# Rows of negated maxima in a fused attention block: written by a DMA per head instead of by products with the identity

## The chip, the cores and the metric

The kernel runs on one core of one Trainium2 chip. The metric is the device time of one execution in microseconds (us).

## The reference

One transformer block over a batch of 8 sequences of 256 tokens with 128 features, and a context of 8 x 1601 tokens with 96 features:

```python
attn_in = _adaln(x, cond, ...)                       # layer norm, scaled and shifted by cond
x = _attn(attn_in, attn_in, sa_wq, sa_wkv, sa_wo, sa_bo) + x
cross_in = _adaln(x, cond, ...)
ctx_n = _ln(context, ca_lnc_w, ca_lnc_b)
x = _attn(cross_in, ctx_n, ca_wq, ca_wkv, ca_wo, ca_bo) + x
ffn_in = _adaln(x, cond, ...)
x = gelu(ffn_in @ ff_w1 + ff_b1) @ ff_w2 + ff_b2 + x

# _attn: 16 heads of 64
q, k = _rope(q, sq, cq), _rope(k, sk, ck)
sim = einsum('bhnd,bhmd->bhnm', q, k) * DH ** (-0.5)
o = einsum('bhnm,bhmd->bhnd', softmax(sim), v)
```

The softmax takes the maximum of each query's scores away before the exponential. The kernel computes that maximum for every query and head.

## The kernel before, in words

All data stay on the chip with features on partitions. The work goes in **steps**: a step J is one sequence and one pair of heads. There are 64 steps of self-attention (class of settings `SELF`) and then 64 of cross-attention (`CROSS`), eight steps (the eight pairs) to a sequence. After them comes the feed-forward part.

What each engine does in a step, and in which order, is written by hand as a string of words (lines 83 to 97). A word names an action; a digit behind it is a part of the step (a chunk of 512 keys, a unit of 2 tiles of 124 keys); `+n` says that the action is done for the step n ahead of the current one, `+-1` for the one behind. Each engine runs its words strictly in order; semaphores tie the engines together. The five strings are those of TensorE, VectorE, ScalarE, GpSimd and SyncE, in that order. SyncE does nothing but issue transfers.

The words that matter here, with their lines:

- `t`, `c`, `r` in self-attention (VectorE, lines 918 to 938) are the rotation of queries and keys. `t` multiplies the projected values by the sines into `turned`; SyncE's word `x` (`self_swap`, line 473) swaps neighbouring rows of `turned` into `swapped` with two transfers SBUF to SBUF; `r` adds `swapped` to get the rotated `QK`. In cross-attention the same is `kt`, `kc`, `ka` with SyncE's `k` for the keys, and `qt`, `qc`, then `qa` on GpSimd, with SyncE's `q` for the queries.
- `w` (SyncE, line 463 and 494) loads the projection weights of a later step, two transfers; `wo` in cross-attention loads output weights, one.
- `a` (TensorE, lines 1172 and 1310) computes scores with queries on the partitions of PSUM, for the maximum alone. VectorE reduces them: in self-attention `am` writes `nmx` (line 942), the negated maxima with queries on partitions; in cross-attention `am0` to `am6` write parts and `nm` writes `nmxc` (line 1044).
- `m` (TensorE, `max_rows`, lines 1184 and 1332) turns these into rows. Four products with the identity, the maxima broadcast over 64 columns as weights, write each head's 256 negated maxima into the PSUM bank `XB`, on 64 partitions alike. ScalarE's word `mr` (`rows_of_max`) copies the bank to `MX`.
- `s` (TensorE, lines 1193 and 1343) computes the scores proper, with keys on the partitions, in three products of high and low parts, and a fourth that adds the negated maximum: `share`, filled with 1/64, times `MX`. ScalarE's `e` takes the exponential.
- `p`, `sum`, `o` (TensorE) are the products with the values, the sum of the exponentials and the output projection. GpSimd adds the exponentials up (`c1` to `c6` and `cf` in cross-attention) before `sum`. In self-attention `o` does work only at the last step of a sequence, 16 products at once (line 1249).
- The bank `XB` serves `m`, `sum` and `o` in turn, in cross-attention also `q` and `v`. `x_free` makes each wait for the reader of the use before it.

`RAMP` strings and `RAMP_*` tables say which words of the first cross-attention steps are done in the last ones of self-attention.

Of the kernel before, what the change touches and what calls it, by code (L numbers as in the profile page):

```python
# [12 lines left out]
D = 128  # L13
# [11 lines left out]
class Stage:  # L25


    def __init__(self, name, pe, dve, act, pool, sp, xuses=("m", "sum", "o")):
# [14 lines left out]
class Cross(Stage):  # L43


    def __init__(self, name, rows, keys, tile, chunk, pe, dve, act, pool, sp):
        super().__init__(name, pe, dve, act, pool, sp, ("q", "v", "m", "sum", "o"))
# [18 lines left out]
def block_kernel(nc, xT_in, cT_in, ctx_in, cols_in, cols96_in, ada_in, packs, w1_in, w2_in,  # L66
# [22 lines left out]
    CROSS = Cross("ca", DC, M, 124, 512,  # L89
# [11 lines left out]
    with ExitStack() as ctx:  # L101
# [38 lines left out]
        nmx = sb("nmx", [D, 2, 2])  # L140
        mxc = sb("mxc", [D, 2, 2, len(CROSS.chunks)])
        nmxc = sb("nmxc", [D, 2, 2])
# [80 lines left out]
        class SelfSteps:  # L223

            def __init__(self, a):
                n = a.name
                self.w = [sem(f"{n}_weights_loaded{i}") for i in range(UNROLL)]
                self.wo = sem(n + "_wo_loaded")
                self.qk = sem(n + "_projected")
                self.t = sem(n + "_turned")  # L230
                self.c = sem(n + "_cosines")
                self.swap = [sem(f"{n}_swapped{i}") for i in range(SLOTS)]
                self.r = sem(n + "_rotated")
                self.h = sem(n + "_high")
# [5 lines left out]
                self.mt = sem(n + "_max_rows")  # L240
                self.mr = sem(n + "_max_rows_copied")
                self.s = sem(n + "_scores")
                self.e = sem(n + "_exp")
                self.pv = sem(n + "_pv")
                self.oe = sem(n + "_o_read")
                self.f = sem(n + "_fold")
                self.sum = sem(n + "_sum")
                self.inv = sem(n + "_sum_inverse")
                self.ot = sem(n + "_o_scaled")
                self.y = sem(n + "_y")  # L250
                self.added = sem(n + "_added")

        class CrossSteps:

            def __init__(self, a):
# [22 lines left out]
                self.mt = sem(n + "_max_rows")  # L278
                self.mr = sem(n + "_max_rows_copied")
# [95 lines left out]

        def halves(tile):
            return tile.rearrange("p (a n) -> p a n", n=N)
# [38 lines left out]

        RAMP_PE = {61: "k0", 62: "k1 q0", 63: "k2"}
# [38 lines left out]
        def _(sp):  # L456
# [31 lines left out]
            run_steps(SELF, in_order(SELF.sp, {"w": self_weights, "x": self_swap}))  # L488
# [30 lines left out]

            def cross_weights_of(J, _):  # L520
                cross_weights(J, J % PAIRS)
# [4 lines left out]
            do = {"q": swap_q, "k": swap_k, "w": cross_weights_of, "wo": cross_out_weights_of}  # L526
            ramp = "w w+1 k0 k1 q k2"
            run_ramp(ramp, do)
            run_steps(a_, in_order(a_.sp, do, ahead(ramp)))
# [12 lines left out]
        def _(pool):  # L542
# [11 lines left out]
            pool.memset(share[:, :].bitcast(F32), 1.0 / DH).then_inc(s_rows, 1)  # L554
# [146 lines left out]
        def _(act):  # L701
# [26 lines left out]
            def self_attention(do):  # L728
# [11 lines left out]
                def rows_of_max(J, _):  # L740
                    wait(act, z.mt, J + 1)
                    wait(act, z.s, J - 1)
                    copy(MX[J % 2][:, :], XB[:, 0:N]).then_inc(z.mr, 1)

# [44 lines left out]
                words = {"cn": context_squares, "ca": context_out, "h": high_parts, "ve": read_v, "mr": rows_of_max,  # L789
# [3 lines left out]
            def cross_words():  # L793
# [21 lines left out]
                def rows_of_max(J, _):  # L815
                    wait(act, x.mt, times(J, 1) + 1)
                    wait(act, x.s, times(J, NU) - NU)
                    copy(MX[J % 2][:, :], XB[:, 0:N]).then_inc(x.mr, 1)

# [13 lines left out]
                do = {"qh": high_q, "kh": high_k, "ve": read_v, "mr": rows_of_max, "e": exponentials, "oe": read_o}  # L833
                return do

            def cross(do):
# [5 lines left out]
                ramp = ("table0 square0 kh2 square1 kh3 ve0 square2 ve1 root0 mr table1 e0 ve2 e1 kh0+1 out0 qh+1 e2 "  # L842
# [23 lines left out]
            act.wait_ge(s_rows, 3)  # L866
# [5 lines left out]
        def _(dve):  # L872
# [44 lines left out]
            def self_attention(do):  # L917
# [21 lines left out]
                def maximum(J, _):  # L939
                    wait(dve, z.a, J + 1)  # L940
                    wait(dve, z.mt, J)
                    dve.tensor_reduce(nmx[:, :, :], MP[:, :, :].rearrange("p h (t n) -> p h t n", n=N), AX.X, ALU.max,  # L942
                                      negate=True).then_inc(z.am, 1)
# [37 lines left out]
            def cross_words():  # L981
# [59 lines left out]
                def maximum(J, _):  # L1041
                    wait(dve, x.am, times(J, NM) + NM)
                    wait(dve, x.mt, times(J, 1))
                    dve.tensor_reduce(nmxc[:, :, :], mxc[:, :, :, :], AX.X, ALU.max, negate=True
                                      ).then_inc(x.nm, 1)
# [46 lines left out]
        def _(pe):  # L1092
# [26 lines left out]
            RAMP = ("a0 zsum0 zp0 a1 mean0 mean1 k3 a2 zo0 a3 var0 a4 var1 mean2 v0 a5 v1 var2 a6 m k0+1 s0 v2 q+1 s1 k1+1 "  # L1119
# [20 lines left out]
            def self_attention(do):  # L1140
# [3 lines left out]
                readers = {"m": (z.mr, lambda K, k: K + 1),  # L1144
                           "sum": (z.ot, lambda K, k: K + 1),
# [108 lines left out]
                words = {"qk": project, "v": project_v, "a": max_scores, "m": max_rows, "s": scores, "p": products,  # L1254
# [4 lines left out]
            def cross_words():  # L1259
# [4 lines left out]
                           "m": (x.mr, lambda K, k: K + 1), "sum": (x.ot, lambda K, k: K + 1),  # L1264
# [47 lines left out]
                def max_scores(J, u):  # L1312
# [11 lines left out]
                    for t in range(2) if last else (u % 2,):  # L1324
                        for h in range(2):
                            at = t * N if last else 0
                            ins = pe.matmul(MP[:, h, at:at + w], QH[J % UNROLL][half(h), t * D:(t + 1) * D],  # L1327
                                            KH[J % 2][half(h), lo:lo + w], start=True, stop=True)
                    ins.then_inc(x.mp, 1)

                def max_rows(J, _):
                    wait(pe, x.nm, times(J, 1) + 1)
                    x_free(uses, readers, J, ("m", 0))
                    for t in range(2):
                        for h in range(2):
                            ins = pe.matmul(XB[half(h), t * D:(t + 1) * D],
                                            nmxc[:, t, h:h + 1].broadcast_to([D, DH]), ident[:, :],
                                            start=True, stop=True)
                    ins.then_inc(x.mt, 1)

                def scores(J, c):
                    r, i = J % UNROLL, J % 2
                    wait(pe, x.kl, times(J, NK) + a_.chunk_of(c) + 1)
                    if c == 0:
                        wait(pe, x.ql, times(J, 1) + 1)
                        wait(pe, x.mr, times(J, 1) + 1)
# [36 lines left out]
                def output(J, _):  # L1383
# [4 lines left out]
                    for h in range(2):  # L1388
# [4 lines left out]
                      "m": max_rows, "s": scores, "p": products, "sum": sums, "o": output}  # L1393
# [87 lines left out]
            pe.wait_ge(s_rows, 3)  # L1481
# [61 lines left out]
```

## Time and profile before

| | |
|---|---|
| median of 3 runs | 1983.65 us (1982.58 to 1987.21) |
| the profiled execution, its own time | 1985.08 us |
| its span in the trace | 1983.3 us |
| mean granted clock of TensorE | 0.991 of full |
| TensorE busy | 1915.2 us (97%) |
| VectorE busy | 1570.7 us (79%) |
| GpSimd busy | 1265.8 us (64%) |
| ScalarE busy | 984.3 us (50%) |
| transfers issued by SyncE | queue busy 17.8% of 16 engines' span |

Names in the profile: PE is TensorE, PEld its weight load, DVE VectorE, ACT ScalarE, POOL GpSimd, SP SyncE (SPq its queue of transfers). The span runs from the first to the last instruction; the profiled execution's time is 1.8 us more. A busy share is a mean over stages that are limited by different things.

### The profile page before, as it was taken

The page shows a single profiled execution, that of the slowest core. Times are in us where ns is not written, and L with a number is a line of the kernel's source. Part 1 is how long each engine was busy: PE and PEld are TensorE (multiplying, and loading weights), DVE is VectorE, ACT ScalarE, POOL GpSimd, SP SyncE. Part 2 cuts the span into 40 slices and gives each one's busy share as a digit, 9 for nine tenths or more (in the row PEclk, how much of TensorE's full clock was granted, in tenths as well). Part 3 has the DMA queues.
Part 4 walks back from the last instruction along what each step waited for, and adds up shares of the span by engine and source line. Part 5 has one row for each costly group of instructions (what it writes and reads, how often), then busy time and mean ns, then how long its engine had stood idle before and what let it go on. Part 6 is the DMA issues. An engine that isn't in the chain of part 4 may idle for free.

```text
span 1983.3 us, 53782 instructions
## 1 busy us (share of the span) xinstructions
PE 1915.2 (97%) x20840; PEld 1327.3 (67%) x20840; DVE 1570.7 (79%) x2291; ACT 984.3 (50%) x1587; POOL 1265.8 (64%) x819
## 2 busy tenths in 40 slices
PE   6989998988999999999999999999999999999998
PEld 3666776754667767666676766666676677676663
DVE  4888888887888888888888888888888888888852
ACT  3555555544544545544455454445445445555455
POOL 6667655423676766667677667666766766766662
PEclk8999999998999999999999999999999999999999
DMA  5222223211111111111111111111111111111110
GB/s 192 76 83 77 76 82 102 76 50 48 50 50 56 51 56 58 49 49 50 56 51 59 55 50 50 55 52 55 57 51 50 50 55 52 56 58 49 46 35 22
DMA packets 110871, 118.90 MB, mean 60 GB/s; under 512 B 26528, under 2 KB 74784, under 8 KB 110624
## 3 DMA queue, kind: packets, MB, share of 16 engines
q1 hardware_dynamic: 110624, 115.46, 17.8%
q8 instruction: 173, 2.83, 0.6%
q14 instruction: 74, 0.61, 0.1%
HBM read 36.71 MB, written 1.05 MB: 19 GB/s over the span
## 4 chain that ended last, share of the span: by engine, by line
PE 77%; POOL 6%; DMA 6%; DVE 5%; issue 3%; SPq 1%; ACT 1%; DVEq 0%; POOLq 0%; ACTq 0%
PE S L1356 19%; PE OB L1370 17%; PE PB L1295 9%; PE PB L1308 8%; PE S L1327 7%; POOL psum_acc L682 4%; DMA swapped<-turned 4%; DMA qswapped<-qturned 2%; PE PB L1379 2%; PE PB L1280 2%; PE OB L1231 1%; PE PB L1249 1%; PE S L1203 1%; PE PB L1389 1%; DVE nmx L942 1%
## 5 line engine op out<-in xcount | busy, mean ns | idle before, releaser
L682 POOL TENSOR_TENSOR psum_acc<-psum_acc,P 124x1024 f32<-124x1024 f32 (+1 forms) x320 | 690.2, 2157 | 113.7 <-ACT P L825 96.5
L825 ACT ACTIVATE P<-S 124x1024 f32<-124x1024 f32 (+1 forms) x448 | 431.7, 964 | 462.8 <-PE S L1356 461.0
L1039 DVE TENSOR_REDUCE mxc<-S 128x2 f32<-128x1024 f32 x384 | 468.7, 1221 | 85.6 <-PE S L1327 85.0
L1370 PE MATMUL OB<-P,V 124*64 124x256 f32 (+1 forms) x3328 | 428.5, 381 | 0.0
L675 POOL TENSOR_TENSOR psum_acc<-P 124x1024 f32<-124x1024 f32 x64 | 152.4, 2381 | 318.8 <-ACT P L825 318.8
L1370 PEld LDWEIGHTS OB<-P,V 124*64 124x64 f32 (+1 forms) x3328 | 223.5, 136 | 132.5 <-issue 38.6
L1356 PE MATMUL S<-QH,KH 64*124 64x256 f32 (+1 forms) x1664 | 254.5, 302 | 1.7 <-ACT P L825 1.7
L703 ACT ACTIVATE V<-PB 124x512 f32<-124x512 f32 (+1 forms) x320 | 156.7, 490 | 172.1 <-PE PB L1169 83.2
L1004 DVE TENSOR_TENSOR turned<-PB,rope 128x512 f32<-128x512 f32 (+1 forms) x256 | 146.0, 570 | 118.7 <-PE PB L1295 118.5
L1356 PE MATMUL S<-QH,KL 64*124 64x256 f32 (+1 forms) x1664 | 234.4, 277 | 0.0
L1356 PE MATMUL S<-MX,share 64*124 64x256 f32 (+1 forms) x1664 | 234.4, 277 | 0.0
L1356 PE MATMUL S<-QL,KH 64*124 64x256 f32 (+1 forms) x1664 | 234.4, 277 | 0.0
L1308 PE MATMUL PB<-kv_w,ctxT_all 96*64 96x128 f32 (+2 forms) x3328 | 231.5, 276 | 0.0
L1356 PEld LDWEIGHTS S<-QH,KH 64*124 64x124 f32 (+1 forms) x1664 | 153.7, 181 | 108.4 <-issue 108.2
L1308 PEld LDWEIGHTS PB<-kv_w,ctxT_all 96*64 96x64 f32 (+2 forms) x3328 | 185.3, 134 | 58.3 <-issue 37.4
L1295 PE MATMUL PB<-ctxT_all,kv_w 96*64 96x512 f32 (+1 forms) x1024 | 222.9, 514 | 0.9 <-DVE KL L1025 0.6
L1327 PE MATMUL S<-KH,QH 64*128 64x512 f32 (+1 forms) x1024 | 199.8, 407 | 10.2 <-DVE mxc L1039 7.1
L1017 DVE TENSOR_TENSOR PB<-PB,swapped 128x512 f32<-128x512 f32 (+1 forms) x256 | 147.7, 577 | 59.5 <-DMA swapped<-turned 58.2
L1356 PEld LDWEIGHTS S<-QH,KL 64*124 64x124 f32 (+1 forms) x1664 | 154.6, 182 | 12.2
L703 ACT ACTIVATE KH<-PB 128x512 fp32r<-128x512 f32 (+1 forms) x256 | 128.4, 502 | 61.8 <-DVE PB L1017 61.2
L1356 PEld LDWEIGHTS S<-MX,share 64*124 64x124 f32 (+1 forms) x1664 | 154.7, 181 | 0.0
L1356 PEld LDWEIGHTS S<-QL,KH 64*124 64x124 f32 (+1 forms) x1664 | 154.4, 181 | 0.0
(169 smaller groups left out, 2999.3 us busy)
## 6 DMA issues: line engine op xcount, KB each, us to landing
swapped<-turned SPq DMA_DIRECT2D x512, 128.0 KB, 2.1
kv_w<-sa_kv_dram SPq DMA_DIRECT2D x64, 128.0 KB, 2.3
qswapped<-qturned SPq DMA_DIRECT2D x128, 64.0 KB, 1.9
kv_w<-ca_kv_dram SPq DMA_DIRECT2D x64, 96.0 KB, 2.2
ctxT_all<-ctx_dram SPq DMA_DIRECT2D x8, 624.0 KB, 5.1
q_w<-sa_wq_dram SPq DMA_DIRECT2D x64, 64.0 KB, 2.0
q_w<-ca_wq_dram SPq DMA_DIRECT2D x64, 64.0 KB, 2.0
o_w<-ca_wo_dram SPq DMA_DIRECT2D x64, 64.0 KB, 2.0
```

What stands on the lines that cost most here:

```text
L675: pool.tensor_tensor(acc, P_of(J, 0)[0:rows], P_of(J, 1)[0:rows], ALU.add).then_inc(x.acc, 2)
L682: pool.tensor_tensor(acc, acc, P_of(J, c)[0:rows, :, 0:w], ALU.add).then_inc(x.acc, 1)
L703: return act.activation(out, in_, ACT.Copy)
L825: act.activation(P_of(J, c)[0:rows, :, 0:w], SP[0:rows, :, 0:w], ACT.Exp, scale=SCALE).then_inc(x.e, 1)
L1004: dve.tensor_tensor(turned[c][:, 0:w], KB[c % 2][:, 0:w], rope[:, M + lo:M + lo + w], ALU.mult).then_inc(x.kt, 1)
L1017: dve.tensor_tensor(KB[c % 2][:, 0:w], KB[c % 2][:, 0:w], swapped[c][:, 0:w], ALU.add).then_inc(x.ka, 1)
L1039: dve.tensor_reduce(mxc[:, t, :, c:c + 1], MP[:, :, 0:w], AX.X, ALU.max).then_inc(x.am, 1)
L1295: ins = pe.matmul(KB[c % 2][half(h), 0:w], kv_w[J % UNROLL][0:DC, half(h)], ctxT_all[0:DC, at:at + w], start=True, stop=True)
L1308: ins = pe.matmul(XB[a:b, k * PAIR:(k + 1) * PAIR], ctxT_all[0:DC, lo + a:lo + b], kv_w[J % UNROLL][0:DC, PAIR:2 * PAIR], start=True, stop ...
L1327: ins = pe.matmul(MP[:, h, at:at + w], QH[J % UNROLL][half(h), t * D:(t + 1) * D], KH[J % 2][half(h), lo:lo + w], start=True, stop=True)
L1356: ins = pe.matmul(SP[0:w, h, k * N:(k + 1) * N], keys[half(h)], queries[half(h), :], start=(n == 0), stop=(n == len(terms) - 1))
L1370: ins = pe.matmul(OB[half(h), 0:N], Vb[J % 2][0:w, t, half(h)], P_of(J, c)[0:w, h, k * N:(k + 1) * N], start=(t == 0), stop=(t == len(a_.t ...
```

## The change

`max_rows` on TensorE, its copy `rows_of_max` on ScalarE, and their two semaphores go, in both stages. In their place SyncE has a new word `mx`: for each of the two heads one transfer from `nmx` (or `nmxc`), 128 partitions with two numbers each, into one row of `MX` of 256 numbers, on partition 0 or 64. So that the two numbers of a partition are neighbours in the row, the maximum scores are computed with queries 2p and 2p+1 on partition p: the weights of `a` are read with a step of two (`t::2`) in place of 128 queries in a row. `share` becomes 1.0 and the other rows of `MX` are zeroed once, so that the fourth product of `s` adds one row. `nmx` and `nmxc` get two buffers each. The words `w`, `w+1` and `k0` of SyncE's first cross-attention steps move into the last self-attention steps.

```diff
     SELF = Stage("sa",
-                 "qk+3 v+2 sum+-1 p+-1 s a+2 ct m+1 o+-1 n",
+                 "qk+3 v+2 sum+-1 p+-1 s a+2 ct o+-1 n",
                  "r+2 am+1 t+3 rc+-1 dv+-1 c+3 ad+-1 cn n",
-                 "e mr+1 ca cn ve+3 h+3 oe",
+                 "e ca cn ve+3 h+3 oe",
                  "l+2 cp f cq",
-                 "w+3 x+2")
+                 "w+3 x+2 n+1 mx+1")
     CROSS = Cross("ca", DC, M, 124, 512,
-                  "a3 k0+1 v3+-1 p1+-1 a4 s3+-1 q+1 p2+-1 a5 s4+-1 v0 n0 k1+1 s5+-1 a6 v1 n1 k2+1 p3+-1 m n2 "
+                  "a3 k0+1 v3+-1 p1+-1 a4 s3+-1 q+1 p2+-1 a5 s4+-1 v0 n0 k1+1 s5+-1 a6 v1 n1 k2+1 p3+-1 n2 "
...
-                  "e3+-1 e4+-1 ve0 kh0+1 e5+-1 ve1 qh+1 mr n0 kh1+1 e6+-1 ve2 n1 e0 oe+-1 kh2+1 e1 n2 e2 "
+                  "e3+-1 e4+-1 ve0 kh0+1 e5+-1 ve1 qh+1 n0 kh1+1 e6+-1 ve2 n1 e0 oe+-1 kh2+1 e1 n2 e2 "
...
-                  "w+2 k3 k0+1 q+1 k1+1 wo k2+1")
+                  "w+2 k3 k0+1 q+1 k1+1 mx wo k2+1")
...
+        def max_to_rows(sp, negated, rows, semaphore):
+
+            for h in range(2):
+                sp.dma_start(rows[h * DH:h * DH + 1, :].bitcast(F32),
+                             negated[:, h, :].bitcast(F32)).then_inc(semaphore, 16)
...
+            def self_max(J, _):
+                wait(sp, z.am, J + 1)
+                wait(sp, z.s, J - 1)
+                max_to_rows(sp, nmx[J % 2], MX[J % 2], z.mr[J % 2])
...
+            def cross_max(J, _):
+                wait(sp, x.nm, J + 1)
+                wait(sp, x.s, times(J, NU) - NU)
+                max_to_rows(sp, nmxc[J % 2], MX[J % 2], x.mr[J % 2])
...
-            pool.memset(share[:, :].bitcast(F32), 1.0 / DH).then_inc(s_rows, 1)
+            pool.memset(share[:, :].bitcast(F32), 1.0).then_inc(s_rows, 1)
+            for i in range(2):
+                pool.memset(MX[i][:, :].bitcast(F32), 0.0).then_inc(s_rows, 1)
...
-                            ins = pe.matmul(MP[:, h, t * N:(t + 1) * N], high(J, 0, t * D, t * D + D)[half(h)],
+                            ins = pe.matmul(MP[:, h, t * N:(t + 1) * N], high(J, 0, 0, N)[half(h), t::2],
                                             high(J, 1, 0, N)[half(h)], start=True, stop=True)
...
-                def max_rows(J, _):
-                    wait(pe, z.am, J + 1)
-                    x_free(uses, readers, J, ("m", 0))
-                    for t in range(2):
-                        for h in range(2):
-                            ins = pe.matmul(XB[half(h), t * D:(t + 1) * D],
-                                            nmx[:, h, t:t + 1].broadcast_to([D, DH]), ident[:, :],
-                                            start=True, stop=True)
-                    ins.then_inc(z.mt, 1)
...
                 def scores(J, _):
                     wait(pe, z.l, J + 1)
-                    wait(pe, z.mr, J + 1)
+                    wait(pe, z.mr[J % 2], J // 2 * 32 + 32)
```

The order of SyncE's transfers in a self-attention step, before (names: `swapped<-turned` is the word `x`, `kv_w` and `q_w` the word `w`):

```order
L477 DMA swapped<-turned 64x512 [waits sa_turned]
L477 DMA swapped<-turned 64x512
L467 DMA kv_w<-sa_kv_dram 128x256 [waits sa_v_projected]
L468 DMA q_w<-sa_wq_dram 128x128
L477 DMA swapped<-turned 64x512 [waits sa_turned]
L477 DMA swapped<-turned 64x512
```

and in the changed kernel (`MX<-nmx` is the new word `mx`):

```order
L482 DMA swapped<-turned 64x512 [waits sa_turned]
L482 DMA swapped<-turned 64x512
L377 DMA MX<-nmx 1x128x2 [waits sa_scores,sa_max]
L377 DMA MX<-nmx 1x128x2
L472 DMA kv_w<-sa_kv_dram 128x256 [waits sa_v_projected]
L473 DMA q_w<-sa_wq_dram 128x128
L482 DMA swapped<-turned 64x512 [waits sa_turned]
L482 DMA swapped<-turned 64x512
```

Two transfers that wait for the maximum now stand between a step's swaps and the weight loads, and so ahead of the next step's swaps. VectorE's order around them did not move (before; `nmx` is `am`, `turned` is `t`, `QK` is `r`):

```order
L937 TENSOR_TENSOR QK<-PB,swapped 128x512 [waits sa_low,sa_swapped0,sa_cosines]
L942 TENSOR_REDUCE nmx<-S 128x4 [waits sa_max_rows,sa_max_scores]
L924 TENSOR_TENSOR turned<-PB,ropeq 128x512 [waits sa_rotated,sa_swapped1,sa_projected]
L947 RECIPROCAL PB<-PB 128x256 [waits sa_sum]
L953 TENSOR_TENSOR oTs<-oraws,PB 128x256 [waits sa_y,sa_o_read,sa_sum_inverse]
L930 TENSOR_TENSOR PB<-PB,ropeq 128x512 [waits sa_turned]
```

Only the semaphore that `nmx` waits for is another one. In a cross-attention step SyncE's order in the changed kernel is this:

```order
L518 DMA qswapped<-qturned 64x256 [waits ca_q_turned]
L518 DMA qswapped<-qturned 64x256
L526 DMA swapped<-turned 64x512 [waits ca_k_turned]
L526 DMA swapped<-turned 64x512
L377 DMA MX<-nmxc 1x128x2 [waits ca_scores,ca_max]
L377 DMA MX<-nmxc 1x128x2
L512 DMA o_w<-ca_wo_dram 128x128 [waits ca_y]
L526 DMA swapped<-turned 64x512 [waits ca_k_turned]
L526 DMA swapped<-turned 64x512
L504 DMA kv_w<-ca_kv_dram 96x256 [waits ca_v_projected]
L505 DMA q_w<-ca_wq_dram 128x128
```

The two new transfers stand ahead of the output weights and of the swap of the third chunk of keys; the rest is as before.

## Rows read from the trace of the kernel before

**Rows 1.** The page: busy time by engine, and the chain that ended last, by engine.

```profile
PE 1915.2 (97%) x20840; PEld 1327.3 (67%) x20840; DVE 1570.7 (79%) x2291; ACT 984.3 (50%) x1587; POOL 1265.8 (64%) x819
PE 77%; POOL 6%; DMA 6%; DVE 5%; issue 3%; SPq 1%; ACT 1%; DVEq 0%; POOLq 0%; ACTq 0%
```

**Rows 2.** The chain of waits, 150 to 162 us: start, duration, what.

```profile
154.33 1.21 DVE nmx L942
155.54 0.61 DVE turned L924
156.15 0.02 issue
156.17 0.47 SPq L477
156.64 0.04 issue
156.68 2.08 DMA swapped<-turned
...
159.52 1.21 DVE nmx L942
```

**Rows 3.** Timeline of SyncE, 150 to 167 us: start, duration, issues.

```profile
156.17 1.11 SPq L477 DMA_DIRECT2D swapped<-turned  x2
157.32 0.58 SPq L467 DMA_DIRECT2D kv_w<-sa_kv_dram  x1
157.95 0.46 SPq L468 DMA_DIRECT2D q_w<-sa_wq_dram  x1
```

**Rows 4.** Timeline of VectorE, self-attention: the reductions to `nmx`.

```profile
59.89 1.21 DVE L942 TENSOR_REDUCE nmx<-S 128x4 f32<-128x1024 f32 x1
...
133.92 1.22 DVE L942 TENSOR_REDUCE nmx<-S 128x4 f32<-128x1024 f32 x1
...
143.94 1.21 DVE L942 TENSOR_REDUCE nmx<-S 128x4 f32<-128x1024 f32 x1
...
412.56 1.23 DVE L942 TENSOR_REDUCE nmx<-S 128x4 f32<-128x1024 f32 x1 [0.30 <-PE PB L1188]
```

**Rows 5.** The chain of waits, 134 to 147 us, at the end of a sequence.

```profile
138.01 0.67 PE PB L1188 x8
138.68 0.02 issue
138.70 0.39 ACT MX L703
139.10 0.14 issue
139.23 3.69 PE PB L1249 x32
```

**Rows 6.** The chain of waits, 1000 to 1024 us, in cross-attention.

```profile
1019.54 0.86 PE OB L1370 x8
1020.41 0.44 PE PB L1336 x8
1020.85 0.43 PE S L1327 x2
```

**Rows 7.** Timeline of VectorE, cross-attention: two reductions to `nmxc`, and a swap waited for.

```profile
510.84 0.17 DVE L1044 TENSOR_REDUCE nmxc<-mxc 128x4 f32<-128x16 f32 x1
...
1018.70 0.17 DVE L1044 TENSOR_REDUCE nmxc<-mxc 128x4 f32<-128x16 f32 x1
...
1023.04 0.70 DVE L1017 TENSOR_TENSOR PB<-PB,swapped 128x512 f32<-128x512 f32 x1 [0.43 <-DMA swapped<-turned]
...
1894.29 0.17 DVE L1044 TENSOR_REDUCE nmxc<-mxc 128x4 f32<-128x16 f32 x1
```

**Rows 8.** Timeline of TensorE, a cross-attention step: first products of `s0`.

```profile
1023.91 0.28 PE L1356 MATMUL S<-QH,KH 64*124 64x256 f32 x2
1024.03 0.28 PE L1356 MATMUL S<-QH,KL 64*124 64x256 f32 x2
```

**Rows 9.** GpSimd's last addition and TensorE's `sum`, in two cross-attention steps.

```profile
560.65 1.27 POOL L682 TENSOR_TENSOR psum_acc<-psum_acc,P 113x512 f32<-113x512 f32 x1
563.05 0.65 PE L1379 MATMUL PB<-psum_acc,onesw 124*64 124x256 f32 x4
...
586.26 0.65 PE L1379 MATMUL PB<-psum_acc,onesw 124*64 124x256 f32 x4 [0.18 <-POOL psum_acc L682]
```

**Rows 10.** Waits of `sum` for GpSimd: total us, times, longest.

```profile
PEld PB L1379 <- POOL psum_acc L682: 6.2, 13, 0.9
PE PB L1379 <- POOL psum_acc L682: 3.1, 8, 0.7
```

**Rows 11.** Issues of transfers: KB each, median us to landing.

```profile
swapped<-turned SPq DMA_DIRECT2D x128, 16.2 KB, 1.8
```

**Rows 12.** The tile `qswapped`: landing of its 128 transfers, min, median, max.

```profile
DMA to landing us min/median/max: 1.7/1.9/3.7
```

**Rows 13.** Weight loads by form: busy us, mean ns.

```profile
L1327 PEld LDWEIGHTS S<-KH,QH 64*128 64x128 f32 x1024 | 92.0, 184 | 86.7 <-issue 63.4 <-ACT KH L703 23.3
```

More of the change, by code:

```diff
@@ L25, with __init__ @@
 class Stage:
-    def __init__(self, name, pe, dve, act, pool, sp, xuses=("m", "sum", "o")):
+    def __init__(self, name, pe, dve, act, pool, sp, xuses=("sum", "o")):
         self.name = name
@@ L46, in __init__ @@
     def __init__(self, name, rows, keys, tile, chunk, pe, dve, act, pool, sp):
-        super().__init__(name, pe, dve, act, pool, sp, ("q", "v", "m", "sum", "o"))
+        super().__init__(name, pe, dve, act, pool, sp, ("q", "v", "sum", "o"))
         self.rows, self.keys, self.tile = rows, keys, tile
@@ L139, in block_kernel @@
         psum_acc = sb("psum_acc", [D, 2, W])
-        nmx = sb("nmx", [D, 2, 2])
+        nmx = [sb(f"nmx{i}", [D, 2, 2], F32R) for i in range(2)]
         mxc = sb("mxc", [D, 2, 2, len(CROSS.chunks)])
-        nmxc = sb("nmxc", [D, 2, 2])
+        nmxc = [sb(f"nmxc{i}", [D, 2, 2], F32R) for i in range(2)]
         oraw = sb("oraw", [PAIR, N])
@@ L239, in __init__ @@
                 self.am = sem(n + "_max")
-                self.mt = sem(n + "_max_rows")
-                self.mr = sem(n + "_max_rows_copied")
+                self.mr = [sem(f"{n}_max_rows{i}") for i in range(2)]
                 self.s = sem(n + "_scores")
@@ L277, in __init__ @@
                 self.nm = sem(n + "_max")
-                self.mt = sem(n + "_max_rows")
-                self.mr = sem(n + "_max_rows_copied")
+                self.mr = [sem(f"{n}_max_rows{i}") for i in range(2)]
                 self.s = sem(n + "_scores")
@@ L524, in cross_out_weights_of @@
                 cross_out_weights(J, J % PAIRS)
[L526 to L527 removed]
+            do = {"q": swap_q, "k": swap_k, "mx": cross_max, "w": cross_weights_of,
+                  "wo": cross_out_weights_of}
+            run_steps(SELF, in_order(SELF.sp, {"w": self_weights, "x": self_swap, "mx": self_max,
+                                               "n": in_ramp(RAMP_SP, do)}))
+            ramp = "k1 q k2 k3 mx"
             run_ramp(ramp, do)
[L529 removed]
+            run_steps(a_, in_order(a_.sp, do, ahead(*RAMP_SP.values(), ramp)))
             sp.wait_ge(x.ka, NK * STEPS)
@@ L813, in read_v @@
                          XB[0:w, 0:len(ts) * PAIR].rearrange("p (t n) -> p t n", n=PAIR)).then_inc(x.ve, 1)
[L815 to L818, printed above, removed]
                 def exponentials(J, c):
@@ L940, in maximum @@
                     wait(dve, z.a, J + 1)
-                    wait(dve, z.mt, J)
-                    dve.tensor_reduce(nmx[:, :, :], MP[:, :, :].rearrange("p h (t n) -> p h t n", n=N), AX.X, ALU.max,
+                    wait(dve, z.mr[J % 2], J // 2 * 32)
+                    dve.tensor_reduce(nmx[J % 2][:, :, :], MP[:, :, :].rearrange("p h (t n) -> p h t n", n=N), AX.X, ALU.max,
                                       negate=True).then_inc(z.am, 1)
@@ L1042, in maximum @@
                     wait(dve, x.am, times(J, NM) + NM)
-                    wait(dve, x.mt, times(J, 1))
-                    dve.tensor_reduce(nmxc[:, :, :], mxc[:, :, :, :], AX.X, ALU.max, negate=True
+                    wait(dve, x.mr[J % 2], J // 2 * 32)
+                    dve.tensor_reduce(nmxc[J % 2][:, :, :], mxc[:, :, :, :].rearrange("p t h c -> p h t c"), AX.X,
+                                      ALU.max, negate=True
                                       ).then_inc(x.nm, 1)
@@ L1142, in self_attention @@
                 uses = x_uses(SELF)
-                readers = {"m": (z.mr, lambda K, k: K + 1),
-                           "sum": (z.ot, lambda K, k: K + 1),
+                readers = {"sum": (z.ot, lambda K, k: K + 1),
                            "o": (z.added, lambda K, k: batch(K) + 1 if K % PAIRS == PAIRS - 1 else None)}
@@ L1263, in cross_words @@
                 readers = {"q": (x.qc, lambda K, k: K + 1), "v": (x.ve, lambda K, k: K * NV + k + 1),
-                           "m": (x.mr, lambda K, k: K + 1), "sum": (x.ot, lambda K, k: K + 1),
+                           "sum": (x.ot, lambda K, k: K + 1),
                            "o": (x.added, lambda K, k: K + 1)}
@@ L1326, in max_scores @@
                             at = t * N if last else 0
-                            ins = pe.matmul(MP[:, h, at:at + w], QH[J % UNROLL][half(h), t * D:(t + 1) * D],
+                            ins = pe.matmul(MP[:, h, at:at + w], QH[J % UNROLL][half(h), t::2],
                                             KH[J % 2][half(h), lo:lo + w], start=True, stop=True)
                     ins.then_inc(x.mp, 1)
[L1331 to L1339, printed above, removed]
                 def scores(J, c):
@@ L1345, in scores @@
                         wait(pe, x.ql, times(J, 1) + 1)
-                        wait(pe, x.mr, times(J, 1) + 1)
+                        wait(pe, x.mr[J % 2], J // 2 * 32 + 32)
                         if J == 0:
@@ L1392, in cross_words @@
                 do = {"q": project_q, "k": project_k, "v": project_v, "a": max_scores,
-                      "m": max_rows, "s": scores, "p": products, "sum": sums, "o": output}
+                      "s": scores, "p": products, "sum": sums, "o": output}
                 return do
```

20 lines of the change are left out of this document (8 added, 12 removed).

## The prediction
> **What bounds the kernel now.** I read the page first: TensorE is busy 97% of the span, and 77% of the chain that ended last is its work [rows 1]. That looks like a kernel in which every product removed is time gained. But the share is a mean over two stages, so the chain of waits comes next, once in each.
>
> In self-attention the chain does not run through TensorE at all. From one reduction to `nmx` to the next it goes: reduction 1.21 us, `turned` 0.61, SyncE's issue 0.02 + 0.47 + 0.04, landing of the second swap transfer 2.08, and 0.76 from there to the next `nmx` (semaphore, `QK`, semaphore) [rows 2]. The sum is 5.19 us, and that is the distance of the two `nmx` rows (159.52 - 154.33). TensorE is only nearly as long. From the fifth to the second-last `nmx` there are 352.7 us and 58 intervals [rows 4]. Seven of them cross the end of a sequence (the one shown is 10.02 us, the longest 11.10, together 73.7). The other 51 have 278.9 us, 5.47 each: the 5.19 of the loop and 14.2 us of scatter in all.
>
> In cross-attention the chain is TensorE, back to back [rows 6]. Sixty intervals between `nmxc` rows take 1383.5 us, 23.06 each [rows 7]. There a product removed is time gained, as long as nobody else is late.
>
> **The change in self-attention.** Read SyncE's new order against that loop. The swaps of step J+3 used to be issued as soon as `turned` of J+3 was there, because the weight loads of that turn were already out. In the new order `mx` of J+1 waits for `nmx` of J+1, which VectorE writes just ahead of `turned` of J+3; and behind `mx` stand the two weight loads, and only then the swaps. SyncE issues in order, so the swaps start at the end of `nmx` plus four issues. In the loop, `turned` and its 0.02 (0.63 us) are covered by that, and in their place stand the issues:
>
> - Two transfers `mx`: two swaps took SyncE 1.11 us, a `kv_w` 0.58 and a `q_w` 0.46 [rows 3]. The trace has no transfer of 8-byte pieces; the nearest rows say 1.11 for two, and bounds for one are 0.43, the shortest issue, and 0.60. I take 1.11.
> - The two weight loads, until now issued in SyncE's spare time: from 157.32 to 158.41, 1.09 us [rows 3].
> - 0.02 ahead and 0.04 behind each pair: 0.10.
>
> That is 2.30 in place of 0.63: **+1.67 us, a loop of 6.86 us**. Times 51: +85.2 us. Of the 14.2 us of scatter I take half to vanish, being waits of others that a longer loop covers: -7. If none or all of it does, the sum moves by 7 either way.
>
> At the end of a sequence the chain is another one: `m` waits for the bank, 138.01, ScalarE copies it, and the 16 products of `o` start only at 139.23 [rows 5]. Without them `o` can start at 138.01: 1.22 us less, eight times, -9.8. The swaps run beside `o`, so SyncE's delay is hidden there. The first four steps (ahead of the 58 intervals, with context loads in SyncE's queue too) and the first cross-attention step, which now waits for a transfer at its `s0`: together +6, an estimate by the same sums. Self-attention: 85.2 - 7 - 9.8 + 6 = **+74**.
>
> Removing `m` from a normal self-attention step, 0.44 us of TensorE, gives nothing: the swap loop covers it. Neither does ScalarE's copy. The landing of `mx` itself is no matter there: `s` of the step comes behind `v`, which waits for the next `QK`, which comes some 5.6 us after `nmx` (2.30 + 0.47 + 0.04 + 2.08 + 0.7).
>
> **The change in cross-attention.** `m` holds TensorE 0.44 us in a step [rows 6]: at most 64 x 0.44 = 28 us. What is late next? `sum` waits for GpSimd's last addition. In a usual step that ends at 561.92 and `sum` starts at 563.05, 1.13 us of room [rows 9]; but in some, whose query swap landed late, `sum` waits already, 13 times by the longer list [rows 10]. These give nothing, and neither do those that come within 0.44 of it; I take 18 of 64. The other 46 give 20 us. **-20**.
>
> Is the row there in time? `nmxc` ends at 1018.87, SyncE's second issue would start about 1019.45, and `s0` begins at 1023.91, or 1023.47 without `m` [rows 7, 8]. It has 4.0 us to land. Small swaps (16.2 KB) land in 1.8 us [rows 11], query swaps in 1.7 to 3.7 [rows 12]. So it is hidden, nearly always. SyncE's third key swap moves behind two issues and the output weights, 0.4 us later than before; VectorE waits 0.43 for that swap now [rows 7] and would wait 0.8, but it is busy only 79% of the span [rows 1] and catches up before its next result is wanted: nothing. ScalarE's 0.39 us of copy is spare time.
>
> The weights of `a` are read with a step of two. Nothing in the trace is read so. Such loads take 184 ns each and run under the products ahead of them [rows 13]: nothing if the step costs nothing; if it doubles a load, and all of it shows, half of 0.1 us for each of 16 loads and 64 steps, some 50 us (an estimate: pairs of products of 256 columns with such loads follow each other every 0.12 us, at 1023.91 and 1024.03 for instance [rows 8], so a load costs 0.06 at most). I take nothing, because a load of a pair goes under a product pair of 0.2 us. The Trainium skill bears on this too (SBUF — State Buffer, Door 1: lines of 16 bytes are read at full rate if two accesses or more fall into each): by it a step of two fp32 numbers is just free. No row shows it.
>
> **The sum.** 1985.1 (the profiled execution's own time) + 74 - 20 = **2039 us**. That execution lies 1.4 us above the median of the runs shown, which is within the scatter.
>
> **Rivals.**
>
> 1. *Faster: SyncE's issues cost little, so the loop stays.* If an issue held up what is behind it for less than 0.16 us (0.63 / 4), self-attention would gain its 9.8 us and no more, cross-attention 20 to 28: about 1950 us. The point from which the whole change is no loss lies at some 0.3 us an issue: four then cost 1.2, 0.55 more than `turned`, 28 us over 51 steps, as much as is gained. For it: an issue's row need not mean that the queue behind it is held. Against it: 156.17 to 158.41 is four issues back to back at 0.43 and more each, none overlapping [rows 3]. The Trainium skill (DMA: Bandwidth & Descriptors, Anatomy of one DMA, a table for transfers from GpSimd) gives a sequencer some 50 ns for a dispatch; by that figure this rival would hold, and the rows of SyncE speak against it. Chance 6%, of which 1 in 6 ends within 0.2%.
> 2. *The burst slows the swaps.* Six transfers now leave within 3.4 us, and the swaps queue behind 192 KB of weights and 256 small pieces. If they land 1 us later, +51: 2090 us. Against it: `kv_w` leaves 0.04 us behind 256 KB of swaps today. Chance 12%.
> 3. *Small pieces land late.* Beyond 4.0 us `s0` waits. At 5 us, +1.0 in each cross-attention step: 64 us and the gain of 20 is kept: 2103 us. Chance 6%.
> 4. *The weights with a step cost.* Up to 50 us: 2089. Chance 8%.
> 5. *The change doesn't do what it says:* `share` of ones times one row still is a product of the same size, so `s` is as long as before in every case; nothing hangs on this.
>
> **How the numbers follow.** The forecast holds 68%, between 2010 and 2065: the bounds of an issue (0.43 with gaps: four take 1.88, -0.42 x 51 = -21), the scatter (7), and the cross-attention gain (0 to 28). Rivals 2 to 4 lie above it, 26%, and are smaller more often than they are as large as worked out, so that the range to **2080** takes in half of them. Below, **2012** leaves out rival 1. Faster by over 0.2% (what a measurement of this kernel can tell from no change) 5%, within 0.2% 1%, slower 94%.
>
> **What would show it.** In the profile after: `nmx` rows 6.9 us apart in self-attention, with `MX`, `kv_w`, `q_w` and `swapped` back to back in SyncE's timeline and the chain running SPq, DMA, `QK`, `nmx` without `turned`; TensorE idle in `v` for `QK` over 1 us a step; ends of a sequence 8.8 us long; `nmxc` rows 22.6 us apart, and more waits of `sum` for GpSimd than 13; no wait of `s` for `MX` but the first. The prediction is wrong if `nmx` rows stay near 5.2 us (rival 1), if swaps land in 3 us (2), if `s0` waits for a transfer (3), or if `a`'s rows and weight loads lengthen (4).

## The result and the profile after

The changed kernel takes 2069.21 us (median of 4 runs, 2067.5 to 2070.8) beside 1985.15 us of the kernel before, measured together: a ratio of 1.0425, 95% interval 1.0409 to 1.0440. It is slower by 84 us. The forecast was 2039 with a range of 2012 to 2080: the sign and the mechanism of the loss held, the loss was half as large again as forecast.

The page of the changed kernel: busy time by engine, TensorE's granted clock in 40 slices, and the chain by engine. They answer to [rows 1].

```profile
PE 1898.0 (92%) x19816; PEld 1282.8 (62%) x19816; DVE 1564.0 (76%) x2291; ACT 939.0 (45%) x1459; POOL 1266.4 (61%) x821
PEclk7999999999799999999999999999999999999999
PE 58%; POOL 13%; issue 12%; DVE 6%; DMA 5%; SPq 5%; ACT 0%; POOLq 0%; DVEq 0%; ACTq 0%
```

TensorE has 1024 records fewer and 17 us less to do, and is busy for a smaller share of a longer span. SyncE's queue has gone from 1% to 5% of the chain: there the time was lost. GpSimd has gone from 6% to 13%: there most of the gain of the removed products went. The largest growth is that of "issue", from 3% to 12%; under this name stands time for which the view names no releaser, and the lines below show that part of it is the landing of a swap.

**Self-attention.** The chain of waits of the changed kernel, 150 to 168 us: start, duration, what. It answers to [rows 2].

```profile
155.54 1.23 DVE nmx L950
156.77 0.02 issue
156.78 0.50 SPq L377
157.28 0.04 issue
157.32 0.70 SPq L377
158.03 0.04 issue
158.07 0.59 SPq L472
158.66 0.04 issue
158.70 0.44 SPq L473
159.14 0.04 issue
159.18 0.50 SPq L482
159.68 0.04 issue
159.72 0.38 DMA swapped<-turned
160.10 1.78 issue
161.89 0.70 DVE QK L945
```

The reader should see that `turned` is no longer in it. (The last two steps before `QK`, 0.38 and 1.78, are one wait: the second swap transfer is issued at 159.72, its landing is on record at 161.81, and `QK` starts at 161.89.) From the end of `nmx` SyncE issues two rows of maxima (L377), `kv_w` (L472), `q_w` (L473) and then the swap (L482), back to back; the swap lands, `QK` follows, and the next `nmx`. In most steps the reductions stand 6.86 us apart (the median is 6.87), the sum that was worked out:

```profile
310.84 1.22 DVE L950 TENSOR_REDUCE nmx<-S 128x4 fp32r<-128x1024 f32 x1
318.16 1.22 DVE L950 TENSOR_REDUCE nmx<-S 128x4 fp32r<-128x1024 f32 x1
...
372.25 1.20 DVE L950 TENSOR_REDUCE nmx<-S 128x4 fp32r<-128x1024 f32 x1
379.10 1.22 DVE L950 TENSOR_REDUCE nmx<-S 128x4 fp32r<-128x1024 f32 x1
```

379.10 - 372.25 is 6.85, the common interval; 318.16 - 310.84 is 7.32, one of the scattered ones: there the second issue of `MX` took 1.1 us instead of 0.60. An end of a sequence takes 8.80 us at the least, as forecast (10.02 before), but several take 9.3 to 10.7.

**Cross-attention.** The second and the last `nmxc`, changed kernel, answering to [rows 7]:

```profile
577.10 0.17 DVE L1052 TENSOR_REDUCE nmxc<-mxc 128x4 fp32r<-128x16 f32 x1
...
2000.98 0.17 DVE L1052 TENSOR_REDUCE nmxc<-mxc 128x4 fp32r<-128x16 f32 x1
```

These 62 intervals take 1423.9 us. In the trace of before the same two rows stand at 486.77 and 1915.92: 1429.2 us. That is 5 us gained, not 20. Of the 62, 18 are at most 22.65 us and 36 are 22.8 to 23.9; a usual one was 22.98 before.

The 62 intervals before, and then after: the stretch, its length, busy us of PE, PEld, DVE, ACT and POOL with their records, the granted clock, the DMA share and GB/s.

```profile
486.77:1915.92 1429.15, 1424.02 (x16104) 993.88 (x16102) 1158.95 (x1790) 710.89 (x1115) 977.44 (x557) 1.00 0.16 53
577.10:2000.98 1423.88, 1406.27 (x15610) 966.38 (x15606) 1153.25 (x1790) 686.77 (x1053) 978.96 (x558) 1.00 0.17 53
```

TensorE has 17.8 us less to do there, and is idle for 17.6 us instead of 5.1: 12.5 of the 17.8 went into new idle time.

TensorE's waits in that stretch, 577 to 2001 us, changed kernel (total us, times, longest): L1367 is `sum`, L1377 is `o`. They answer to [rows 10].

```profile
PEld PB L1367 <- POOL psum_acc L700: 17.8, 25, 1.4
PE PB L1367 <- POOL psum_acc L700: 12.2, 20, 1.2
PEld PB L1377 <- issue: 13.1, 22, 0.9
PE PB L1377 <- DVE oT L1064: 4.3, 11, 0.5
```

`sum` waited for GpSimd 3.1 us in its products' rows before and waits 12.2 now. `o` waiting for `oT` is new.

Where the 84.7 us between the two spans (2068.0 - 1983.3) lie, cut at the same rows in both traces:

| stretch | before | after | difference |
|---|---|---|---|
| start to first `nmx` | 33.5 | 32.5 | -1.0 |
| its first 4 intervals | 26.4 | 36.8 | +10.4 |
| its next 58 intervals | 352.7 | 429.9 | +77.3 |
| from there to the second `nmxc` | 74.2 | 77.9 | +3.7 |
| 62 intervals of `nmxc` | 1429.2 | 1423.9 | -5.3 |
| the rest | 67.4 | 67.0 | -0.4 |

(The cut of the 58 intervals is the 63rd `nmx`, at 412.56 in [rows 4] and 499.22 after.)

### The profile page after: what moved, and what is told of

It reads as the page before. It is cut to its first block, busy times and chain, and to the rows that moved or that the text cites. A ratio compares the mean times of both kernels' runs of the same rounds, so it can differ in the third digit from the quotient of the medians.

```text
span 2068.0 us, 51734 instructions
## 1 busy us (share of the span) xinstructions
PE 1898.0 (92%) x19816; PEld 1282.8 (62%) x19816; DVE 1564.0 (76%) x2291; ACT 939.0 (45%) x1459; POOL 1266.4 (61%) x821
## 4 chain that ended last, share of the span: by engine, by line
PE 58%; POOL 13%; issue 12%; DVE 6%; DMA 5%; SPq 5%; ACT 0%; POOLq 0%; DVEq 0%; ACTq 0%
PE S L1344 15%; PE OB L1358 14%; PE PB L1293 7%; POOL psum_acc L700 7%; PE PB L1306 6%; PE S L1325 6%; DMA qswapped<-qturned 4%; DVE nmx L950 2%; SPq L377 2%; PE PB L1367 2%; PE PB L1377 2%; POOL psum_acc L666 1%; POOL psum_acc L705 1%; DMA swapped<-turned 1%; POOL KL L659 1%
## 5 line engine op out<-in xcount | busy, mean ns | idle before, releaser
L1325 PE MATMUL S<-KH,QH 64*128 64x512 f32 (+1 forms) x1024 | 204.0, 414 | 8.2 <-DVE mxc L1047 5.7
L659 POOL TENSOR_TENSOR KL<-QK,KH 128x512 fp32r<-128x512 f32 x64 | 82.0, 1281 | 192.3 <-ACT KH L721 192.3
L1344 PEld LDWEIGHTS S<-QH,KL 64*124 64x124 f32 (+1 forms) x1664 | 155.6, 182 | 12.2
L1325 PEld LDWEIGHTS S<-KH,QH 64*128 64x128 f32 x1024 | 96.2, 192 | 98.2 <-issue 81.6
```

What stands on the lines that cost most here:

```text
L1344: ins = pe.matmul(SP[0:w, h, k * N:(k + 1) * N], keys[half(h)], queries[half(h), :], start=(n == 0), stop=(n == len(terms) - 1))
```

## The experiments

The ratios are to the kernel before on the same chip. Its medians were 1986.87 us (runs 1 to 4), 1989.44 (runs 5 to 8) and 1987.45 (run 9 and the repeat of run 6).

**1. The transfers of maxima behind the swaps (self-attention only).**

```diff
-                 "w+3 x+2 n+1 mx+1")
+                 "w+3 x+2 mx n+1")
```

> The changed kernel with one word of SyncE's self-attention order moved: the transfers of the maxima of step J leave behind the swaps of J+2, where s of J is still about 2.5 us away, so that they no longer stand between a maximum and the next swaps. Theory A (the loop is the sum of SyncE's issues between nmx and the swaps): nmx rows come back to 5.2 us apart, ends of a sequence stay at 8.8 us, TensorE's clock stays up in the ramp. Self-attention loses 71.5 us of the increase and 8 of the ends, the first steps and the ramp up to 18: about 1971 us, below the kernel before. Theory B (the burst or the small pieces slow the swaps' landing wherever they stand): nmx rows 6 us or more apart, the time above 2010 us.

Measured: 1982.12 us, ratio 0.9976 (0.9963 to 0.9989). One word moved and the whole loss is gone. The chain of waits of this run, 150 to 165 us, is that of [rows 2] again, with `turned` in it:

```profile
150.07 0.61 DVE turned L932
150.68 0.02 issue
150.70 0.49 SPq L482
151.19 0.04 issue
151.24 2.11 DMA swapped<-turned
...
154.05 1.22 DVE nmx L950
```

`nmx` rows are 5.19 us apart, ends of a sequence 8.79 to 9.9, and the 58 intervals take 347.0 us: 5.7 less than before the change. The same six transfers leave SyncE within a step, so it is their order that cost, not their number or size. Theory B falls. The first four intervals, 36.8 us in the changed kernel, are 28.0 again. The time is still 11 us above what A gave: cross-attention is not better than in the changed kernel (62 intervals in 1426.9 us), and the ramp, from the 63rd `nmx` to the second `nmxc`, stays at 78.0 us. Theory A had TensorE's clock stay up in the ramp; the granted clock there was 0.85, against 0.91 before the change.

**2. The third key swap ahead of the output weights too.**

```diff
-                  "w+2 k3 k0+1 q+1 k1+1 mx wo k2+1")
+                  "w+2 k3 k0+1 q+1 k1+1 mx k2+1 wo")
```

> As the run before, and in cross-attention the third key swap goes ahead of the output weights, directly behind the two transfers of maxima. Theory A (the late third key swap delays ka2, the maximum behind it and the reciprocal, until o waits for oT): waits of o for oT go, some steps of 23.2 us fall to 22.6, 4 to 10 us less than the run before, 1961 to 1967. Theory B (only the late query swaps and GpSimd's additions behind them hold the cross-attention steps): no difference over 3 us.

Measured: 1981.48 us, 0.9970 (0.9956 to 0.9984), 62 intervals in 1425.0 us. That is Theory B's answer: no difference. Waits of `o` for `oT` fell from 5.9 to 3.3 us, while those of `sum` for GpSimd went from 12.1 to 13.8.

**3. Two of the four issues taken out of the loop.**

```diff
-                 "w+3 x+2 n+1 mx+1")
+                 "x+2 w+4 n+1 mx+1")
```

> The changed kernel with SyncE's weight loads ahead of the maxima in self-attention, the maxima still ahead of the swaps. Theory A by the sum of issues: the loop loses 1.09 + 0.04 us, nmx rows 5.73 us apart instead of 6.86; 51 steps give 58 us, the clock in the ramp up to 8 more: 2003 to 2012 us. Theory B (the wait for the maximum in SyncE's queue costs, not the number of issues behind it): nmx rows stay above 6.3 us, the time above 2035.

Measured: 2017.48 us, 1.0157 (1.0136 to 1.0178). The chain, 150 to 165 us:

```profile
154.42 0.02 issue
154.43 0.50 SPq L377
154.94 0.04 issue
154.98 0.60 SPq L377
155.58 0.04 issue
155.63 0.60 SPq L482
156.22 0.04 issue
```

`nmx` rows stand mostly 5.81 to 5.87 us apart: 1.0 us less than 6.86 for two issues fewer, near the 1.13 expected (the first swap's own issue is 0.60 here, not 0.50). So the price is that of each issue on SyncE, as the sum had it, and Theory B falls. The 51 normal intervals give back 50 us (363.2 to 313.0) of the 58 expected; the total is 5 us above the expected 2012.

**4. The weights of the maximum scores read in a row.**

```diff
-            high(J, 0, 0, N)[half(h), t::2],
+            high(J, 0, t * D, t * D + D)[half(h)],
...
-                            ins = pe.matmul(MP[:, h, at:at + w], QH[J % UNROLL][half(h), t::2],
+                            ins = pe.matmul(MP[:, h, at:at + w], QH[J % UNROLL][half(h), t * D:(t + 1) * D],
```

> The changed kernel with the weights of the maximum scores read in a row instead of with a step of two; the maxima of other queries are then taken away from a query's scores, so the result differs by what the softmax divides out again. Theory A (a step of two costs nothing): the time of the changed kernel within 3 us, 2066 to 2072. Theory B (loads with a step are slower): the 4 us by which the rows of a grew (204.0 against 199.8 us) come back, the weight loads of a 184 ns instead of 192, 2062 to 2066 us. If loads were doubled and shown, 2019.

Measured: 2076.44 us, 1.0457 (1.0434 to 1.0480). Weight loads by form, this run and then the changed kernel (busy us, mean ns):

```profile
L1325 PEld LDWEIGHTS S<-KH,QH 64*128 64x128 f32 x1024 | 92.4, 184 | 103.7 <-issue 88.0 <-ACT KH L721 15.6
```

```profile
L1325 PEld LDWEIGHTS S<-KH,QH 64*128 64x128 f32 x1024 | 96.2, 192 | 98.2 <-issue 81.6 <-ACT KH L721 16.3
```

The products themselves, this run and then the changed kernel:

```profile
L1325 PE MATMUL S<-KH,QH 64*128 64x512 f32 (+1 forms) x1024 | 200.2, 407 | 13.5 <-DVE mxc L1047 10.6
L1325 PE MATMUL S<-KH,QH 64*128 64x512 f32 (+1 forms) x1024 | 204.0, 414 | 8.2 <-DVE mxc L1047 5.7
```

A load with a step of two takes 8 ns more, and the products of `a` 3.8 us more in the whole span: the rows are those of Theory B. Its time, 2062 to 2066, did not come, nor the 2066 to 2072 of Theory A: the run is even 0.3% slower than the changed kernel's first comparison, and run 8 below shows that two comparisons of the changed kernel differ by more than that. So the step costs some 4 us of TensorE's work, which is more than nothing and too little to be seen in these times; the 50 us of the rival are excluded.

**5. No query swap in cross-attention.** GpSimd adds `qturned` unswapped, so part of the rotation is left out; VectorE's and GpSimd's waits for the transfer go with it. So do two issues of SyncE's in each step, so that this run takes away more than the late landings alone.

```diff
-                  "w+2 k3 k0+1 q+1 k1+1 mx wo k2+1")
+                  "w+2 k3 k0+1 k1+1 mx wo k2+1")
...
-                    wait(pool, x.qswap[i], J // 2 * 32 + 32)
-                    pool.tensor_tensor(qrotb[i][:, :], qrotb[i][:, :], qswapped[i][:, :], ALU.add
+                    wait(pool, x.qt, times(J, 1) + 1)
+                    pool.tensor_tensor(qrotb[i][:, :], qrotb[i][:, :], qturned[i][:, :], ALU.add
```

> The changed kernel without the transfer that swaps the rotated queries' rows in cross-attention: GpSimd adds the unswapped rows (so that part of the rotation is left out), and waits for VectorE alone. Theory A (late query swaps hold GpSimd, its additions hold sum, and that takes the gain of the products removed): nmxc rows 22.6 us apart in nearly all steps, 62 intervals in about 1401 us instead of 1424, the time about 2046 us. Theory B (the late third key swap behind the maxima takes the gain): 10 us of the 23 at most come back, 2058 or more.

Measured: 2070.66 us, 1.0412 (1.0391 to 1.0433). Beside the changed kernel on the same chip (run 8, 2083.07) that is 12 us less; the 62 intervals take 1417.6 us against 1433.4 there, and 1423.9 in the first trace of the changed kernel. TensorE's waits in cross-attention, 577 to 2001 us; `sum` (L1366 here) no longer stands among them, `o` (L1376) does:

```profile
PEld PB L1376 <- issue: 17.2, 24, 0.9
PE PB L1376 <- DVE oT L1063: 7.3, 19, 0.5
```

So two waits share what the products' removal should have brought. The larger is `sum` for GpSimd, because of late query swaps: 12 us of TensorE's idle time in both traces of the changed kernel, none here (the intervals differ by 6 to 16 us, according to the trace compared). The other is `o` for `oT`, 7.3 us here, 4.3 and 5.5 in the two traces. TensorE's idle time in the 62 intervals is 10.6 us here, 17.6 and 25.5 there. That `oT` is late because SyncE issues the third key swap late, as Theory B says, is not shown: run 2 gained nothing by issuing it earlier, and run 9 below keeps the waits.

**6. GpSimd's addition of unit 4 ahead of its wait for the query swap**, with both orders of SyncE's from run 2.

```diff
-                  "c2+-1 c3+-1 qa+1 c4+-1 c5+-1 cf+-1 c6+-1 c1 ql+1",
+                  "c2+-1 c3+-1 c4+-1 qa+1 c5+-1 cf+-1 c6+-1 c1 ql+1",
```

> The run with both orders of SyncE's transfers mended, and GpSimd adds the exponentials of unit 4 before it waits for the query swap instead of after it. Theory A: a swap that lands 1.2 to 2 us late is covered by that addition, sum waits no more, 62 intervals of nmxc take 1401 to 1406 us instead of 1425: 1957 to 1963 us, 1.3% under the kernel before. Theory B: the query words of ScalarE and TensorE that wait for the rotated queries become late instead, gain under 8 us, above 1973.

Measured: 1962.02 us, 0.9871 (0.9851 to 0.9891). This is the version that beats both kernels, by 1.3% the one before and by over 5% the changed one. GpSimd's wait for the query swap in the whole span, this run:

```profile
POOL qrot L677 <- DMA qswapped<-qturned: 33.2, 2, 28.7
```

It waited 64 times and 86.3 us in the changed kernel (32.0 of them at the start), and twice here, both at the start. The 62 intervals take 1412.0 us (478.85 to 1890.85), and `sum` waits for nothing. The 11 us above 62 x 22.6 = 1401 lie in steps of 22.8 to 24.5 us; TensorE's idle time is 7.2 us, and `o` still waits for `oT` in eleven products' rows (4.1 us).

**7. The same reordering in the kernel before.**

> The kernel before with GpSimd's same reordering and nothing else. It tells what of the next best version is not the change's own. Theory A: there the late swaps cost only what exceeds 1.1 us of room, 5 us of the 1429 between nmxc rows: 1980 to 1983 us. Theory B (the swaps cost the kernel before as much as the changed one): 1965 or less.

Measured: 1981.72 us, 0.9965 (0.9953 to 0.9978), 62 intervals in 1423.7 us: 5.5 us less than 1429.2, Theory A. TensorE's idle time there falls from 5.1 to 0.6 us: in the kernel before, the late swaps had no more than that to cost. Of run 6's gain 0.4% is therefore not the change's; the other 0.9% is.

**8. The changed kernel again.**

> The changed kernel once more, beside the others on this chip: 4.2% over the kernel before, 2066 to 2074 us. If it is as slow as the run without the step (4.6%), the difference of those two is scatter of the swaps' landing; if not, reading in a row costs 7 us.

Measured: 2083.07 us, 1.0475 (1.0454 to 1.0495), against 1.0425 the first time. The 62 intervals took 1433.4 us in this profile and 1423.9 in the first. Run 4's 1.0457 lies between: no gain of reading the weights in a row can be told from these times. A difference of 0.5%, some 10 us, between two comparisons of one kernel is the limit of what can be said of it here.

**9. ScalarE issues the transfers of the maxima in cross-attention**, at the place of its former copy; the rest as run 6.

```diff
-                  "w+2 k3 k0+1 q+1 k1+1 mx k2+1 wo")
+                  "w+2 k3 k0+1 q+1 k1+1 k2+1 wo")
...
-                  "e3+-1 e4+-1 ve0 kh0+1 e5+-1 ve1 qh+1 n0 kh1+1 e6+-1 ve2 n1 e0 oe+-1 kh2+1 e1 n2 e2 "
+                  "e3+-1 e4+-1 ve0 kh0+1 e5+-1 ve1 qh+1 mx n0 kh1+1 e6+-1 ve2 n1 e0 oe+-1 kh2+1 e1 n2 e2 "
```

> The run with additions first, and in cross-attention ScalarE issues the transfers of the maxima, at the place where its copy of the bank stood, so that SyncE's queue there is as in the kernel before. Theory A (two issues ahead of the third key swap still cost, by ka2, the reciprocal and oT): waits of o for oT go, 62 intervals of nmxc in 1402 to 1406 us instead of 1412, 6 to 10 us less than that run. Theory B (ScalarE is held by its own issues, 1.1 us against the copy's 0.39, and the keys' high parts and exponentials behind come late): no gain, or up to 10 us lost. Theory C (what is left is the landing of the swaps themselves): within 3 us of that run.

Measured: 1965.27 us, 0.9890 (0.9870 to 0.9910). Beside it stands run 6 repeated on the same chip.

> The run with additions first once more, on the chip of the run with ScalarE's issues: 1.3% under the kernel before, within 0.3%.

That one took 1966.88 us, 0.9888 (0.9873 to 0.9904). Both have 62 intervals in 1411.8 us. Theory C: SyncE's two issues ahead of the third key swap cost nothing once they stand ahead of it alone; what is left is not on SyncE's queue. `o` still waits for `oT` eleven times (4.5 us). Each of these waits comes within 12 us of the landing of a key swap that took more than 2.35 us (2.0 is usual), where only about half of all moments in the stretch do; that the landings are the cause is supported by this, not shown by an experiment.

## Why the prediction was right, and where it was off

- **The loop.** That SyncE's issues between `nmx` and the swaps set the pace of self-attention was right. 5.19 + 1.67 = 6.86 us was forecast, 6.86 is what the rows show; from the end of `nmx` to the first swap's issue it is 2.32 us in most steps (2.30 forecast). Runs 1 and 3 show it by taking four and two issues out of the loop.
- **The scatter was not absorbed.** Half of 14.2 us was to vanish in the longer loop. The 51 normal intervals take 363.2 us, 7.12 each, so 13.3 us remain above 6.86: +6 us against the forecast. It is not the waits of others, as the forecast had it: in 15 of the 17 normal intervals above 7.2 us one issue on SyncE took 1.0 to 1.95 us instead of 0.43 to 0.60. A longer loop cannot cover that, since the loop is made of these issues. The last section says what stands beside the long ones.
- **The ends of a sequence.** -1.22 us each was right in the undisturbed ones (8.80 us). The seven in the stretch take 66.7 us against 73.7, -7.0 for -8.5 forecast.
- **The first steps and the ramp** were put at +6, and with the last end -1.2. They took +13.1 (-1.0 + 10.4 + 3.7). The term was too small by its own rule: four intervals at 1.67 us are 6.7 already, without the context loads. That SyncE's order makes most of the 10.4 is shown by run 1, where these four are 8.8 us shorter. The ramp's 3.7 us are another matter, and there I had not priced TensorE's clock. Windows of the changed kernel (columns as above):

```profile
60.00:160.00 100.00, 70.19 (x696) 49.02 (x696) 72.78 (x86) 37.54 (x61) 55.03 (x53) 0.93 0.22 63
526.00:582.00 56.00, 46.12 (x340) 25.82 (x338) 37.01 (x57) 21.31 (x36) 15.22 (x9) 0.82 0.14 45
```

  Before, the clock was 1.00 from 60 to 160 us, with TensorE busy 90 of 100 us, and 0.91 in the 56 us around the ramp. With 70 of 100 us busy it fell to its lower level in pieces, and the 6.86 us of the loop show nothing of it. In the ramp it does show. Two groups of `s0` there, changed kernel, chain of waits:

```profile
540.36 2.07 PE S L1344 x16
...
554.41 1.14 PE S L1344 x14
```

  Such a group takes 2.07 us where the granted clock is 0.50 (1.2 GHz) and about 1.2 where it is 1.00 (2.4). Over all twelve traces the ramp is by and large the longer the lower its mean granted clock: 73.0 and 74.2 us at 0.91, 74.8 to 75.8 at 0.89, 77.0 to 77.3 at 0.87, 78.0 at 0.85 and 77.9 at 0.82. But the longer loop of self-attention is not shown to be the reason: run 1 has the short loop and 0.85 in the ramp, run 4 the long loop and 0.89, and run 6 and its repeat, one kernel, take 73.0 and 75.7 us. So most of the 3.7 us may be scatter; what sets the clock in the ramp stays open.
- **Cross-attention's -20 was the largest miss**, 15 us. Two terms failed. The smaller is the price of `m`: 0.44 us in each of 62 steps is 27.3 us, and TensorE's work fell by 17.8. The products of `a`, read with a step, grew by about 4 us and those of `s` by about 4; a usual step became shorter by 0.38. The larger is the count of steps without gain: 18 of 64 was forecast, and 36 of 62 stayed at 22.8 us or above. There the 12.5 us of new idle time are. I asked who waited already and who came within 0.44 us, on one path, by the room of a usual step (1.13 us, [rows 9]). In a third of the steps the query swap is late: GpSimd stands idle for it 0.9 us or more in 20 of 62 steps before and in 26 of 62 after, against some 0.3 us usually. For these the room of 1.13 us was being used; with 0.44 of it gone each costs up to 0.44 more than it did. And the second path, a key swap, `ka2`, maximum, reciprocal, `oT`, `o`, I had written off with "catches up": TensorE now comes to `o` early enough to wait, 11 times by the row above. Runs 5, 6 and 7 show the first. For the second, the rows show the waits; SyncE's two issues ahead of the third key swap are not their cause (run 9).
- **Hidden as forecast:** the landing of the rows. 256 pieces of 8 bytes a step land as fast as a swap; the transfers of the tile `MX`, changed kernel:

```profile
DMA to landing us min/median/max: 1.9/2.0/3.9
```

  `s` waited for them once, 2.5 us, at the first cross-attention step. The step of two was hidden but for the 4 us of `a`'s products (run 4).
- **The rivals.** Cheap issues (1): no; most rows hold the queue 0.43 to 0.60 us, the shortest 0.34. The Trainium skill (DMA: Bandwidth & Descriptors, Anatomy of one DMA) gives about 50 ns for the sequencer's dispatch on GpSimd's path; SyncE's rows show nothing so short. The burst (2): no; the swaps' median landing is 2.0 us, and in run 1 the same six transfers in another order leave a loop of 5.19. Small pieces (3): no. Weights with a step (4): 4 us, not 50.
- **How much of it was luck.** The forecast's own terms reached to 2065; the range went on to 2080 to take in half of rivals 2 to 4. None of these came true at the size worked out, and the 2069 measured lies above 2065: it is inside the range because of an allowance for other causes. All four misses, the scatter (+6), the ends (+1.5), the first steps and the ramp (+8) and cross-attention (+15), went the same way, 31 us in all.

## What to carry to other kernels

Before a transfer goes into an in-order queue that only issues, ask what stands behind it and what it waits for: here a word that waited for a reduction stood ahead of transfers whose own loop was the stage's limit, and the weight loads that had been free were pulled into that loop as well. Put the waiting transfer behind the ones that the loop needs, if its reader comes later still. And where the bounding engine gets faster by little, the room of every other path shrinks by as much: look at the late steps, not at the usual ones, before counting the gain. Where a few transfers in one queue are late or slow to issue, look for packets of another queue beside them before taking it for noise.

## What was not expected of the hardware

A transfer of 128 pieces of 8 bytes takes SyncE 0.50 to 0.60 us to issue and 2.0 us to land, no more than one of 64 rows of 2 KB (0.47 to 0.60, and 2.1).

The late swaps and the long issues go together with packets of the queue that the page of the changed kernel lists so (packets, MB, share of 16 engines):

```profile
q8 instruction: 165, 2.70, 0.5%
```

Each of these packets is 16 KB and takes 0.9 to 1.8 us; one comes every 11 us or so, in the kernel before too. Every issue on SyncE longer than 0.9 us overlaps one: 64 of 64 in the changed kernel and 61 of 61 before, beside 109 of the 1316 shorter ones (100 of 1063 before). Of the query swaps that land late, 25 of 26 (19 of 20 before) have such a packet under way between 1.0 us after their first issue begins and 1.9 us after their second does; of the others none of 36 (none of 42 before). A step of 23 us is about twice the distance of these packets, which fits with the late steps coming in groups of three to five, about every tenth step, after the change. That they go together is what the traces show; no run moved these packets, so that they are the cause stays an inference.
